# Slot tables of two top-2 routers: two wide comparisons against one small pair of instructions per product

## The reference

```python
# third feed-forward layer, E = 8
routing_weights = jax.nn.softmax(x @ gate_w.T, axis=-1)
topk_w, topk_i = jax.lax.top_k(routing_weights, 2)
topk_w = topk_w / jnp.sum(topk_w, axis=-1, keepdims=True)
for e in range(8):
    w_e = jnp.sum(jnp.where(topk_i == e, topk_w, 0.0), axis=-1)
    out = out + w_e[:, None] * ((silu(x @ w_gate[e]) * (x @ w_up[e])) @ w_down[e])
...
# fourth feed-forward layer, E = 16, plus two shared experts
probs = jax.nn.softmax(xt @ W_router, axis=-1)
top_v, top_i = jax.lax.top_k(probs, 2)
gate = jnp.sum(jax.nn.one_hot(top_i, 16) * top_v[..., None], axis=1)
routed_out = einsum('ted,edh->th', gelu(xt @ Wrt_up) * gate[:, :, None], Wrt_down)
```

## Time and profile before

| | us |
|---|---|
| time, median of 3 runs | 3114.33 (3113.45 to 3116.43) |
| time of the profiled execution | 3107.09 |
| its span, first to last instruction | 3105.4 |
| mean granted TensorE clock | 0.906 of full speed |
| PE / DVE / ACT / POOL busy | 2389.4 / 2056.9 / 1503.2 / 1075.3 |

### The profile page before, as it was taken

How to read it: one execution, slowest core, us unless ns; L and a number is a source line. 1 busy time by engine, 2 the same in 40 slices (tenths; PEclk the granted TensorE clock), 3 DMA queues, 4 the chain that set the end, 5 groups by cost and what they waited for, 6 DMA issues and landing times. The chain is left out here.

```text
span 3105.4 us, 39908 instructions
## 1 busy us (share of the span) xinstructions
PE 2389.4 (77%) x13100; PEld 1074.2 (35%) x13100; DVE 2056.9 (66%) x3302; ACT 1503.2 (48%) x2076; POOL 1075.3 (35%) x818
## 2 busy tenths in 40 slices
PE   2989997899969934676666489928898888796882
PEld 0542332344434311222222256614422222353551
DVE  6658774545456798999997652246588888456523
ACT  2554554254332765555553353325557777433642
POOL 4766765011001235666664121155541000001224
PEclk9998999899979967889987599968889999998996
DMA  4542221120000000000000462254522100313735
GB/s 157 179 171 86 86 86 66 63 86 1 1 4 13 1 0 1 0 1 0 0 0 28 136 200 86 82 152 155 209 96 82 61 9 15 103 48 130 247 129 194
DMA packets 128413, 245.60 MB, mean 79 GB/s; under 512 B 32515, under 2 KB 59407, under 8 KB 126310
## 3 DMA queue, kind: packets, MB, share of 16 engines
q1 hardware_dynamic: 107094, 169.49, 15.6%
q0 software_dynamic: 21136, 73.68, 7.7%
HBM read 154.24 MB, written 88.60 MB: 78 GB/s over the span
## 5 line engine op out<-in xcount | busy, mean ns | idle before, releaser
L1901 DVE TENSOR_REDUCE ac_nmax<-ac_M 128x1 f32<-128x512 f32 (+1 forms) x768 | 491.6, 677 | 75.4 <-PE ac_M L1734 70.8
L1883 ACT ACTIVATE ac_PT<-ac_S 128x1024 f32<-128x1024 f32 x384 | 388.0, 1021 | 187.4 <-PE ac_S L1761 168.4
L3477 POOL TENSOR_TENSOR sc_hc<-sc_h,sc_cs 128x1024 f32<-128x1024 f32 x128 | 300.5, 2355 | 157.2 <-DVE sc_h L3592 93.0
L3592 DVE TENSOR_TENSOR_SCAN sc_h<-sc_dA,sc_dB 128x1024 f32<-128x1024 f32 x128 | 292.1, 2282 | 12.3 <-ACT sc_dA L3558 12.3
L3512 PE MATMUL sc_y<-sc_hc,ident 128*128 128x512 f32 x512 | 258.0, 631 | 18.6 <-DVE x_res L3608 16.3
L3558 ACT ACTIVATE sc_dA<-ss_delta,sc_A 128x511 f32<-128x511 f32 x256 | 166.0, 682 | 28.8 <-DVE sc_h L3592 28.0
L774 DVE SCALAR_TENSOR_TENSOR mo_y16l<-mo_yT,mo_y16h 128x512 f16<-128x512 f32 x86 | 59.4, 690 | 180.6 <-ACT mo_y16h L717 180.4
L3490 PE MATMUL sc_b<-ss_bc,sc_sel 128*128 128x512 f16 x128 | 53.5, 418 | 154.1 <-DVE sc_dB L3584 122.7
L3584 DVE TENSOR_TENSOR sc_dB<-ss_du,sc_b 128x1024 f32<-128x1024 f32 x128 | 156.1, 1220 | 17.7 <-PE sc_b L3490 6.9
L3563 ACT ACTIVATE sc_cs<-sc_c 128x512 f32<-128x512 f32 x128 | 76.2, 596 | 185.3 <-POOL sc_hc L3477 182.3
L1734 PE MATMUL ac_M<-KT,QT 64*128 64x512 f16 (+1 forms) x384 | 135.7, 428 | 31.9 <-DVE ac_nmax L1901 17.3
(11 more groups left out here) (622 smaller groups left out, 5716.1 us busy)
## 6 DMA issues: line engine op xcount, KB each, us to landing
keys_t<-ap_kto SPq DMA_DIRECT2D x32, 512.0 KB, 2.6
queries_t<-ap_qto SPq DMA_DIRECT2D x32, 512.0 KB, 2.7
slot_results_last<-mo_o SPq DMA_DIRECT2D x47, 256.0 KB
slot_results<-mo_o SPq DMA_DIRECT2D x39, 256.0 KB
values<-ap_vf SPq DMA_DIRECT2D x32, 256.0 KB, 2.9
ac_KT<-keys_t POOLq DMA_DIRECT2D x4, 2048.0 KB, 8.8
ac_QT<-queries_t POOLq DMA_DIRECT2D x16, 512.0 KB, 10.4
attended<-ac_A SPq DMA_DIRECT2D x8, 1024.0 KB, 3.8
```

Source lines behind the costliest of these rows:

```text
L1883: nc.scalar.activation(PT[:, n % PTB, :, :], psS[:, 2 * (n % 2):2 * (n % 2) + 2, :], ACT.Exp, scale=SCALE / (SQK * SQK)).then_inc(exp_done, 1)
L1901: last = v.tensor_reduce(out[:, :, 0], sc[:, 0:MAIN], AX.X, ALU.max)
L3477: nc.gpsimd.tensor_tensor(hc[:, m % RC, :, :], h[:, m % RH, :, :], cs[:, m % 2, :].unsqueeze(1).to_broadcast([P, W, S]), ALU.mult).then_in ...
L3592: nc.vector.tensor_tensor_scan(h[:, m % RH, :, :].rearrange("p c s -> p (c s)"), dA[:, m % 2, :, :].rearrange("p c s -> p (c s)"), dB[:, m ...
```

## The change

Both tables are no longer made by three wide `tensor_tensor` instructions for all 32 columns at once. A new function `spread_slots` makes two small `tensor_scalar` instructions per column n: 128 flags from a fp16 ramp compared with one scalar per partition (`slotf`), and NS values from the same ramp compared with `tile` and multiplied by `tokenf`, both scalars per partition. The ramp of 0 to 127 is now a fp16 tile (`ramp16`, in place of the fp32 `ramp_pf`; lists of instructions print it as `rt_ramp`). None of the small instructions is linked. Each second one increments `placed`, and each of PE's 32 matmuls waits for its own count. `owners` moves up to stand right behind `bases`. In `late_block` the table making is cut in two halves of 16 columns, around `add_shared(LAST + 1)`.

```diff
-        self.tokenf, self.ramp_pf = sb("tokenf", [P, NT]), sb("ramp_pf", [P, P])
+        self.tokenf, self.ramp16 = sb("tokenf", [P, NT]), sb("ramp16", [P, P], F16)
...
-    def spread_within(self, v, c):
-        c.link(v.tensor_tensor(self.hot_p[:], self.ramp_pf[:].unsqueeze(1).to_broadcast([P, 2 * NT, P]),
-                               self.spread(self.slotf[:], P), ALU.is_equal))
-
-    def spread_tiles(self, v, c, placed):
-        NS = self.NS
-        c.link(v.tensor_tensor(self.hot_h[:], self.ramp_pf[:, 0:NS].unsqueeze(1).to_broadcast([P, 2 * NT, NS]),
-                               self.spread(self.tile[:], NS), ALU.is_equal))
-        h4 = self.hot_h[:].rearrange("p (t j) h -> p t (j h)", j=2)
-        v.tensor_tensor(h4, h4, self.tokenf[:].unsqueeze(2).to_broadcast([P, NT, 2 * NS]), ALU.mult).then_inc(placed, 1)
+    def spread_slots(self, v, which, placed):
+
+        within, tile = (a[:].rearrange("p t j -> p (t j)") for a in (self.slotf, self.tile))
+        for n in which:
+            v.tensor_scalar(self.hot_p[:, n, :], self.ramp16[:], within[:, n:n + 1], None, ALU.is_equal)
+            v.tensor_scalar(self.hot_h[:, n, :], self.ramp16[:, 0:self.NS], tile[:, n:n + 1],
+                            self.tokenf[:, n // 2:n // 2 + 1], ALU.is_equal, ALU.mult).then_inc(placed, 1)
...
-            pe.wait_ge(placed, 1)
             for n in range(2 * NT):
+                pe.wait_ge(placed, n + 1)
...
             rt.bases(v, c, p_total[:])
+            rt.owners(v, c, step_expert)
             rt.places(v, c, p_rank[:], slot)
-            rt.spread_within(v, c)
-            rt.spread_tiles(v, c, placed)
-            rt.owners(v, c, step_expert)
+            rt.spread_slots(v, range(2 * NT), placed)
             dve.wait_ge(inverted, 1)
...
             rt.bases(v, c, p_total)
+            rt.owners(v, c, step_expert)
             hidden_low(TB - 1, 2)
             hidden_low(TB - 1, 3)
             rt.places(v, c, p_rank, slot)
             add_shared(LAST)
-            rt.spread_within(v, c)
+            rt.spread_slots(v, range(NT), placed)
             add_shared(LAST + 1)
-            rt.spread_tiles(v, c, placed)
+            rt.spread_slots(v, range(NT, 2 * NT), placed)
             add_shared(LAST + 2)
-            rt.owners(v, c, step_expert)
             add_shared(LAST + 3)
```

More of the change, by code:

```diff
@@ L289, in over_e @@
         return v.unsqueeze(2).to_broadcast([P, NT, self.n_exp])
-    def spread(self, v, n):
-        return v.rearrange("p t j -> p (t j)").unsqueeze(2).to_broadcast([P, 2 * NT, n])
     def shift(self, v, c, logits, shifted):
@@ L454, in _ @@
             c.link(v.tensor_copy(rt.tokenf[:], rt.token[:]))
-            c.link(v.tensor_copy(rt.ramp_pf[:], rt.ramp_p[:]))
+            c.link(v.tensor_copy(rt.ramp16[:], rt.ramp_p[:]))
             dve.wait_ge(logit_done, 1)
```

## The result

The changed kernel takes 3119.51 us, median of 20 runs, against 3113.57 us of the kernel before, median of 20 on the same chip. The ratio is 1.0021, with a 95% interval of 1.0015 to 1.0028: 6.5 us slower, between 4.7 and 8.7, or 0.15 to 0.28%. The profiled execution has a span of 3120.9 us and a granted clock of 0.901, 15.5 us over the one of before. Only part of these 15.5 us belongs to the change, so I read the two places apart from the rest.

What follows compares the result with a forecast made beforehand. DVE's instruction list was taken to bound both places; +5.4 us in the first router and +2.3 in the last block made +7.7, so 3114.33 + 7.7 = 3122.0 us, range 3115.5 to 3127.5.

Steps and rivals of the forecast that it cites:

- slower by over 0.2%: Whole kernel: more than 6.2 us slower, the line for telling a change from none; chance 0.64.
- What bounds the places: Third layer's router and last layer's block: DVE's instruction list decides when the token copy, and so the next work, starts.
- the cover at half the clock: Last block: with PE's clock halved, down ends at 2837.7, products at 2838.9, still covered before the copy at 2839.7.
- The price of a pair: Both tables on DVE: one hot_p plus one hot_h column costs 385 ns in the first router, 390 in the last.
- First router: Third layer's router: owners 1.45, tables 12.3 and tail 0.44, less 8.82 us before, make +5.4 us.
- Last block: Last layer's block: bases-side move of owners saves 2.38 us, yet tables and three add_shared take 14.5 against 12.22: +2.3 us.
- That scalars hide: DVE's tables: scalars per partition hide behind the neighbour, pair below 270 ns, not slower; chance 0.20 for partly or wholly.
- the dear case: DVE's tables: fp16 rate fails or odd widths slow down, pair 420 to 505 ns, +9.8 to +15.2 us; chance 0.17.
- the case of the faster kernel: DVE's tables: pair below 170 ns makes the kernel faster by over 0.2%; chance 0.04.
- Products did not get slower by their waits: PE's products: rival that a wait per product makes PE slower than DVE, some +1 us more; chance under 0.02.
- A sign of being wrong that came up: Other blocks: forecast is wrong if one's time moves by microseconds although no line of it changed.
- the sum of about -6 us: Both places: the errata formula, without a term for scalars, gives a pair of some 170 ns and this sum.

Runs made afterwards that it cites:

- the single wait: The changed kernel with PE waiting once for all 32 columns instead of once per product; ratio 1.0025 to the kernel before.
- Three kernels: Wide fp16 tables, pair index innermost, against the kernel before: one hot_p 0.9996, hot_p in four pieces 0.9988, pieces with hot_h written in the old order 1.0025.
- the kernel in pieces: Wide fp16 tables, pair index innermost, with hot_h first and hot_p in four unlinked pieces of 8 columns; ratio 0.9988 to the kernel before.
- the one with POOL's copy later: Fp16 tables with hot_p in four pieces, plus one wait so POOL's ramp copy starts after DVE's small casts; ratio 0.9982 to the kernel before.
- the one with the fp32 ramp: The changed kernel with ramp16 as an fp32 tile; ratio 1.0037 to the kernel before.
- the one with `owners` behind in the first router: The changed kernel with owners behind the tables again in the first router; one run, first router 16.48 us, last block 23.09 us.
- the first and the third with wide fp16 tables: Wide fp16 tables, pair index innermost: first with one hot_p, 0.9996 of the kernel before; third with hot_p in pieces and hot_h written in the old order, 1.0025.
- `owners` moved alone: The kernel before with owners right behind the bases in the last block only; ratio 0.9998, last block 18.69 us.
- the prices: The kernel before with nine series of eight unlinked tensor_scalar instructions added on DVE of the first router; fp16 103 ns apart with a constant, 163 with one scalar.

## Why the prediction came out right

The forecast was +7.7 us (3122.0), with "slower by over 0.2%" as the likeliest case; measured were +6.5 us and 3119.5. The measured 0.21% sits on the line that the forecast drew, and its interval reaches to both sides of it: that it is slower is shown, that it is over 0.2% isn't.

- *What bounds the places.* Right: DVE's list sets both ends, and in the last block the two `add_shared` cover PE: its last product ends at 2850.43, 0.9 us before the copy. The clock was at its higher level there (1.00 in 2841 to 2851), so the cover at half the clock, which the prediction also claimed, wasn't put to the test. Shown by the single wait too: 1.02 us in the one place; in the other the copy followed the additions again.
- *The price of a pair.* I took 385 and 390 ns; it is 363 and 366 (32 pairs in 11.7 us with the last one's length). The mechanism held part by part: 33 ns of stream for 128 elements at fp16, 60 ns per scalar, 80 ns of overlap. Mis-sized was the fixed part, 160 ns from the 128- and 512-wide rows, where the short rows (my lower bound, 360 ns a pair) gave it: 188 - 33 = 155 ns for one alone with the constant and, from distances, 103 + 80 - 33 = 150 ns. That is 20 ns a pair. `hot_h` streams at the fp16 rate in spite of its odd width, some 10 ns where I took 20 to 25, and its second scalar costs 60 ns and not 52. In 64 pairs this is 1.5 us too much. A wait for PE that I hadn't counted (next point but one) hid a third of that by luck, and the sum came out 1.1 us high.
- *First router.* Forecast +5.4, measured 4.66. The terms: `owners` 1.45 (1.46), tail 0.44 (0.39 counted alike), tables 12.3 (11.6).
- *Last block.* Forecast +2.3, measured +1.94, of which 0.57 is a wait for PE at the lower clock that I had considered only for PE's last `down`. Without it the move of `owners` gave its 2.4 us and the tables took back 3.8.
- *Rivals.* That scalars hide is refuted (163 against 103 ns), and with it the case of the faster kernel. The fp16 rate came, so the dear case fell too. Products did not get slower by their waits. One price among the rivals was added up wrong: without the 172 ns of scalars a pair of 385 ns is 213 and not "about 270", so wholly hidden scalars would have made the kernel 3.5 us faster, where the prediction put them at no change. The forecast doesn't use it.
- *A sign of being wrong that came up.* The prediction named "another block's time moves by microseconds although no line of it changed". The profiled execution did show that, 8.9 us of it. It isn't an effect of the change as far as the runs can tell: the same stretches vary as much between executions of nearly the same code, and the ratio agrees with the two places alone, within its 2 us to either side.
- *The weighing of the page.* The Trainium skill's page "VectorE: DVE Perf Modes", section on the TRN2 errata, has a formula that makes 58 + 32 cycles of such a short instruction, by my estimate 94 ns; measured without a scalar per partition were 103. With scalars its formula falls short by 60 ns each, so the sum of about -6 us made with it was wrong while its advice against small tiles was right.

## What to carry to other kernels

Count instructions before elements: 64 short ones with 96 scalars per partition cost 11.7 us where three wide ones took 7.4, and the pipelining that they bought is bounded by what stood behind them, here 1.1 us in the first router and nothing in the last block. To let a consumer follow, four pieces were enough here: with `owners` behind them the copy in the first router waited for nothing. Moving an instruction into a hole of its engine is free only where there is such a hole: the same move gave 2.4 us in one block and cost 0.4 in the other. And work put on an idle engine isn't free because that engine is idle: look at what its neighbour does in the same microseconds.

## What the runs showed of the hardware that I had not expected

POOL and DVE: while POOL ran a 128x4096 copy from int32 to fp16 (3.60 us), a 32-wide DVE instruction that started 0.7 us into it lasted 2.96 us instead of 0.19, to the copy's end. Three kernels show it, and one wait takes it away. In the head of the last block the same copy (3.61 us) lay where DVE was idle, and cost nothing.

A fp16 write on DVE at a stride of 78 or 94 bytes: 5.47 us for 1248 elements, 7.17 us for 1504, with 160 ns fixed taken off about 4.3 and 4.7 ns per element, against 0.52 without a stride. I expected the loss of the 16-bit rate alone, 1.04. Why it is four times that stays open.

PE's products with both tables at a stride of 64 bytes: 84 ns apart instead of 34 with 39 columns at the lower clock (0.50), 97 instead of 26 with 47 columns at the higher one (1.00).

TensorE's clock in the last block: in the kernel in pieces and in the one with POOL's copy later, the code of the last block is the same, but the busy times by stretch differ (columns as above). In pieces:

```profile
2821.00:2825.00 4.00, 3.39 (x16) 1.58 (x17) 3.73 (x10) 0.00 (x0) 0.00 (x0) 1.00 0.00 0
```

With the copy later:

```profile
2822.00:2826.00 4.00, 3.36 (x9) 1.20 (x10) 3.73 (x9) 0.00 (x0) 0.00 (x0) 0.60 0.00 0
```

After the same 2.1 us without work, PE's `down` starts at the higher clock (2.4 GHz) in one and for some 3.5 us at the lower (1.2 GHz) in the other. It costs 0.5 us where DVE sets the end and 1.7 us where PE does. Six of the eleven profiled executions have the wait for PE, of 0.56 to 0.58 us: the changed kernel, the one with the fp32 ramp, the one with `owners` behind in the first router, the first and the third with wide fp16 tables and the one with POOL's copy later. The kernel before, the single wait, `owners` moved alone, the prices and the kernel in pieces are without it. The same six had the lower clock once before in this block, in the `down` group ahead of the bases. There `add_shared` waits for PE, in the changed kernel and in the kernel before:

```profile
2811.93 0.75 DVE L2379 SCALAR_TENSOR_TENSOR x_res<-la_o,la_cs,x_res 128x512 f32<-128x512 f32 x1 [3.14 <-PE la_o L2211]
2800.13 0.75 DVE L2386 SCALAR_TENSOR_TENSOR x_res<-la_o,la_cs,x_res 128x512 f32<-128x512 f32 x1 [1.61 <-PE la_o L2218]
```

The wait is 3.0 to 3.1 us in the six and 1.6 in the other five; the granted clock is 0.58 in 2808 to 2812 of the changed kernel and 1.00 in the matching 2796.4 to 2800.4 of the kernel before. `owners` and the tables run only after that group, so their new places in this block don't start it. Whether the change makes it likelier in some other way isn't settled: the single wait, with the same code up to there, came without it, and each kernel has one profile.
